# Moving a quarter of the position products into the feed-forward, and the last keys' projection between the first largest scores

## The chip, the cores and the metric

The program runs on one core of one Trainium2 chip. The metric is device time in microseconds of one execution over all eight images. TensorE multiplies matrices into PSUM (eight banks), VectorE, ScalarE and GpSimd work on tiles (GpSimd in SBUF alone here), and SyncE issues transfers. Each engine runs its own list of instructions in order, and semaphores tie the lists together.

## The reference, cut to what matters

```python
# layer 0, for each of 8 images of 32x32 tokens, C = 384, 6 heads of 64
x = x + L0_conv_ref(_gn(x), ...)      # qkv with bias; scores + rel_h + rel_w; softmax; values; projection
# inside: position terms
rel_h = einsum('bhwc,hkc->bhwk', r_q, Rh)
rel_w = einsum('bhwc,wkc->bhwk', r_q, Rw)
attn = attn + rel_h[:, :, :, :, None] + rel_w[:, :, :, None, :]
# layer 1
t = t + L1_attn_ref(_ln_t(t), Wq, Wk, Wv, Wo, bo)      # causal
t = t + L1_ffn_ref(_ln_t(t), ...)                       # kron-factored feed-forward with gelu
```

## The kernel before

Images are worked one after the other, and each has the same stages: values and position products of layer 0, attention 0, its projection and a norm, attention 1, its projection, feed-forward. The head of an image is overlapped with the feed-forward of the image ahead of it: class `Projections` computes the queries and keys of the next image in six *pairs* (two heads each; pairs 0 to 2 queries, 3 to 5 keys), 18 matmuls of 512 columns a pair. Numbers are kept as a high f16 part and a low f16 part: ScalarE writes the high part from PSUM (`pair_high`, L574), VectorE the low part (`pair_low`, L591). GpSimd writes transposed copies of the queries, high and low, for the column positions (`turn_all`, L617, into `hT` and `lT`), since GpSimd can only read what the other two have already put into SBUF.

The feed-forward is a loop of twelve steps. Step i is `ff.up` (two matmuls, L1303) into banks 0 and 1, then the gelu on ScalarE (L1315), which has to end before the next `ff.up`, since both use one bank pair. `FILL` says how many matmuls of the next image's pairs TensorE puts into each step, `HIGHS` after which gelus ScalarE evicts them. After the odd steps from 3 on comes `ff.down` (L1323), and at step 9 a first `ff.spread` (L1337).

The position products (`rel_products`, L653) come in four quarters, n = 0 to 3, of 96 small matmuls, and each fills two banks. ScalarE takes each quarter out in four pieces (`rel_high`, L670) and VectorE in four more (`rel_low`, L676). `with_v` says behind which tile of values (`v_products`, L688 and L693; ScalarE takes a tile out in L700 and L701, GpSimd makes its low part in L705) a quarter stands: 0 to 3, all behind the feed-forward. Two bank pairs alternate, so quarters 2 and 3 wait for the low parts of the quarters before.

Then come the sixteen products of the first head's *largest scores* (L825), one bank each, reduced by VectorE (L971). Their list is `attn0.prologue`, their banks are `ahead`, here four. Next, a row of maxima is turned (L830), copied by VectorE (L979), carried into `qc` by a transfer (L1063), and the first score tile (L861 to L872) and its exponential (L947) follow. The attention then runs at its own pace. Every list is written out by hand in `tensor`, `scalar`, `vector`, `gpsimd` and `sync`.

## Time and profile before

| what | us |
|---|---|
| median of 3 runs | 2881.56 |
| lowest and highest | 2880.02, 2882.01 |
| the profiled execution | 2876.72 |
| its span, first to last instruction | 2874.7 |
| TensorE busy | 2648.2 (92%) |
| ScalarE, VectorE, GpSimd busy | 2047.1, 1987.1, 1734.9 |

Times inside the trace count from the span's start. The kernel has seven boundaries between images; the sixth, around 2130 to 2215 us, is the one read closely below. A busy TensorE is not one at its peak: matmuls overlap, and a matmul's own duration holds some pipeline time.

### The profile page before, as it was taken

The page shows a single profiled execution, that of the slowest core. Times are in us where ns is not written, and L with a number is a line of the kernel's source. Part 1 is how long each engine was busy: PE and PEld are TensorE (multiplying, and loading weights), DVE is VectorE, ACT ScalarE, POOL GpSimd, SP SyncE. Part 2 cuts the span into 40 slices and gives each one's busy share as a digit, 9 for nine tenths or more (in the row PEclk, how much of TensorE's full clock was granted, in tenths as well). Part 3 has the DMA queues.
Part 4 walks back from the last instruction along what each step waited for, and adds up shares of the span by engine and source line. Part 5 has one row for each costly group of instructions (what it writes and reads, how often), then busy time and mean ns, then how long its engine had stood idle before and what let it go on. Part 6 is the DMA issues. An engine that isn't in the chain of part 4 may idle for free.

```text
span 2874.7 us, 69176 instructions
## 1 busy us (share of the span) xinstructions
PE 2648.2 (92%) x29116; PEld 1548.0 (54%) x29116; DVE 1987.1 (69%) x3631; ACT 2047.1 (71%) x2435; POOL 1734.9 (60%) x1181
## 2 busy tenths in 40 slices
PE   7899998999989998999989999899998999989995
PEld 4465644656446563565635656366553655546562
DVE  7776767666775767757677576775777758677574
ACT  6686866858668586785767867678766777668683
POOL 5474764737657376573756746566565665657473
PEclk8999999999999999999999999999999999999998
DMA  3100011000100001000010000200002000010000
GB/s 113 36 2 1 2 34 45 2 1 2 56 23 2 1 2 56 23 2 1 2 57 23 2 1 6 74 2 2 1 9 71 2 2 1 12 45 2 1 2 22
DMA packets 36115, 53.65 MB, mean 19 GB/s; under 512 B 5824, under 2 KB 32704, under 8 KB 35808
## 3 DMA queue, kind: packets, MB, share of 16 engines
q1 hardware_dynamic: 34304, 48.64, 5.5%
q8 instruction: 231, 3.78, 0.5%
q10 hardware_dynamic: 1504, 0.61, 0.1%
q14 instruction: 76, 0.62, 0.1%
HBM read 30.95 MB, written 12.58 MB: 15 GB/s over the span
## 4 chain that ended last, share of the span: by engine, by line
PE 49%; POOL 16%; ACT 13%; issue 11%; DVE 9%; DMA 1%; POOLq 0%; ACTq 0%; DVEq 0%; SPq 0%
POOL pl L1013 15%; PE ps L555 12%; PE ps L902 7%; PE ps L688 4%; PE ps L861 4%; PE ps L872 4%; ACT p L947 4%; PE ps L825 4%; PE ps L1104 4%; DVE mxp L971 3%; PE ps L863 3%; ACT ph L933 3%; ACT qa L670 2%; PE ps L1303 2%; PE ps L1323 2%
## 5 line engine op out<-in xcount | busy, mean ns | idle before, releaser
L1013 POOL TENSOR_TENSOR pl<-p,ph 128x1024 f16<-128x1024 f32 (+2 forms) x672 | 1095.9, 1644 | 384.2 <-ACT ph L933 378.3
L971 DVE TENSOR_REDUCE mxp<-ps 128x1 f32<-128x512 f32 (+2 forms) x1344 | 779.4, 627 | 267.9 <-PE ps L825 263.3
L947 ACT ACTIVATE p<-ps 128x1024 f32<-128x1024 f32 (+1 forms) x672 | 640.3, 953 | 165.8 <-PE ps L872 165.0
L933 ACT ACTIVATE ph<-p 128x1024 f16<-128x1024 f32 (+1 forms) x672 | 669.3, 996 | 21.4
L902 PEld LDWEIGHTS ps<-v,ph 128*128 128x128 f16 x9600 | 506.2, 97 | 128.2 <-issue 27.6
L902 PE MATMUL ps<-v,ph 128*128 128x65 f16 (+1 forms) x9600 | 531.0, 194 | 17.0 <-POOL pl L1013 16.0
L902 PE MATMUL ps<-v,pl 128*128 128x65 f16 x4800 | 509.1, 192 | 0.0
L902 PEld LDWEIGHTS ps<-v,pl 128*128 128x128 f16 x4800 | 446.8, 99 | 0.0
L872 PE MATMUL ps<-qc,kc 65*128 65x512 f16 (+3 forms) x1344 | 380.0, 364 | 0.1
L1013 DVE TENSOR_TENSOR pl<-p,ph 128x512 f16<-128x512 f32 (+1 forms) x336 | 244.2, 727 | 184.3 <-ACT ph L933 183.0
L705 POOL TENSOR_TENSOR v<-o,v 128x384 f16<-128x384 f32 x128 | 116.7, 918 | 411.0 <-ACT o L701 411.0
L861 PE MATMUL ps<-qa,ka 128*128 128x512 f16 x768 | 292.5, 381 | 0.0
L863 PE MATMUL ps<-qb,ka 128*128 128x512 f16 x768 | 291.7, 380 | 0.0
L825 PE MATMUL ps<-ka,qa 128*128 128x512 f16 x768 | 247.1, 383 | 43.9 <-DVE mxp L971 25.1
L700 ACT ACTIVATE v<-ps 128x384 f16<-128x384 f32 x128 | 63.6, 497 | 180.8 <-PE ps L693 107.3
L872 PEld LDWEIGHTS ps<-qc,kc 65*128 65x128 f16 (+1 forms) x1344 | 123.8, 98 | 126.4 <-issue 0.5
L825 PEld LDWEIGHTS ps<-ka,qa 128*128 128x128 f16 x768 | 73.2, 97 | 182.7 <-DVE mxp L971 70.8
L861 PE MATMUL ps<-qa,qb 128*128 128x512 f16 (+1 forms) x576 | 162.0, 344 | 2.1 <-ACT p L947 2.1
L555 PE MATMUL ps<-xin,wqkv_hi 128*128 128x512 f16 x576 | 155.9, 384 | 4.0 <-DVE xin L508 2.2
L825 PE MATMUL ps<-qb,qa 128*128 128x512 f16 (+2 forms) x576 | 154.9, 325 | 0.0
L1000 DVE TENSOR_TENSOR lT<-ps,hT 128x512 f16<-128x512 f32 x96 | 66.4, 692 | 127.5 <-ACT hT L938 127.5
L1315 ACT ACTIVATE p<-ps 128x1024 f32<-128x1024 f32 x96 | 98.0, 1021 | 60.6 <-PE ps L1303 59.5
(187 smaller groups left out, 5075.2 us busy)
## 6 DMA issues: line engine op xcount, KB each, us to landing
xin<-in_x SPq DMA_DIRECT2D x8, 1536.0 KB, 6.9
x<-in_x SPq DMA_DIRECT2D x8, 1536.0 KB, 8.1
out<-x SPq DMA_DIRECT2D x16, 768.0 KB, 4.1
qc<-qa SPq DMA_DIRECT2D x42, 128.0 KB, 2.3
p<-in_L_conv_qkv_w SPq DMA_DIRECT2D x3, 576.0 KB, 10.6
qc<-rowt SPq DMA_DIRECT2D x96, 2.0 KB
x<-in_L_attn_Wq SPq DMA_DIRECT2D x1, 576.0 KB, 7.9
x<-in_L_attn_Wk SPq DMA_DIRECT2D x1, 576.0 KB, 9.0
```

The source lines that it names most:

```text
L555: mm = nc.tensor.matmul(m.ps[:, self.bank[i] + j, :], w[:, k, self.order[i] * P:(self.order[i] + 1) * P], x(k, 4 * j, 4 * j + 4), start=(n ...
L688: mm = nc.tensor.matmul(m.ps[:, 6 + t % 2, 0:C], flat_tile(x(k, t, t + 1)), w[:, k, 2 * C:3 * C], start=(n == 0), stop=(self.layer == 1 an ...
L705: self.nc.gpsimd.tensor_tensor(self.m.v[:, t, :, HD + 1:VW], self.m.o[:, t, :].rearrange("p (h d) -> p h d", d=HD), self.m.v[:, t, :, 0:HD ...
L825: mm = nc.tensor.matmul(m.ps[:, bank, 0:w], m.qa[:, sl, qt * P:(qt + 1) * P], self.ka[:, sl, kh * BANK:kh * BANK + w], start=not diag, sto ...
L861: nc.tensor.matmul(outs[j], self.ka[:, sl, keys[j]], m.qa[:, sl, q], start=True, stop=False)
L863: nc.tensor.matmul(outs[j], self.ka[:, sl, keys[j]], m.qb[:, sl, q], start=False, stop=False)
L872: mm = nc.tensor.matmul(outs[j], m.kc[crows(h), sl, keys[j]], m.qc[crows(h), sl, q], start=False, stop=True)
L902: mm = nc.tensor.matmul(m.ps[:, 6 + half % 2, c0:c0 + w], e, v, start=(first and n == 0), stop=(g in self.last_of_half and n == len(work) ...
L933: self.nc.scalar.activation(m.ph[:, i % RING, :, 0:w], m.p32[:, i % RING, :, 0:w], ACT.Copy).then_inc(self.s["hi"], 1)
L947: nc.scalar.activation(m.p32[:, i % RING, :, 0:w], m.ps[:, 2 * (i % 2):2 * (i % 2) + 2, 0:w], ACT.Exp, scale=SCALE).then_inc(s["exp"], 1)
L971: nc.vector.reduce_max(m.mxp[:, h % 2, kh, qt:qt + 1], m.ps[:, bank, 0:w], AX.X).then_inc(s["free"], 1)
L1013: engine.tensor_tensor(m.pl[:, i % RING, part, 0:w], m.p32[:, i % RING, part, 0:w], m.ph[:, i % RING, part, 0:w], ALU.subtract).then_inc(s ...
```

## The change

For every image but the first:

- Quarter 0 of the position products goes from behind the feed-forward to step 9 of it (`REL_STEP`), ahead of `ff.down`; its four ScalarE pieces go behind gelus 9, 10, 11 and 11 (`REL_HIGHS`), its VectorE pieces between `o2_out` and `widen`.
- Pair 5, the last two heads' keys, leaves the feed-forward (`FILL` has 36 matmuls in place of 54). Its 18 matmuls stand two by two behind the first nine of the sixteen largest-score products. ScalarE writes its high parts and then the whole sums to `p32` (`last_keys_out`), GpSimd its low parts (`last_keys_low`).
- Values tile 5 stands in thirds behind the next three products, tile 6 behind all sixteen.
- The quarters use three bank pairs (`REL_BANK`), and the sixteen products two banks, 0 and 1.
- ScalarE loads the exponential's table ahead of time (`table`).
- GpSimd's first high transposes wait for the queries' high part alone.

```diff
-        self.bank = (4, 6, 2, 4, 2, 4) if layer == 0 else (0, 2, 4, 6, 0, 2)
-        self.before = (0, 0, 0, 2, 6, 8) if layer == 0 else (0, 0, 0, 0, 2, 4)
+        self.bank = (4, 6, 2, 4, 2, 2) if layer == 0 else (0, 2, 4, 6, 0, 2)
+        self.before = (0, 0, 0, 2, 6, 0) if layer == 0 else (0, 0, 0, 0, 2, 4)
...
+    def last_keys_out(self, act):
+        i = 2 * NPAIR - 1
+        f = self.order[i]
+        self.pair_high(act, i)
+        self.nc.scalar.activation(self.held_keys(), self.out2(i), ACT.Identity, bias=self.m.bqk[:, f:f + 1]).then_inc(self.late["whole"], 1)
...
+    def last_keys_low(self, pool, done):
+        m = self.m
+        pool.wait_ge(self.late["whole"], self.late.at("whole", 1))
+        pool.wait_ge(self.s["v_lo"], self.s.at("v_lo", done))
+        for h in (NH - 2, NH - 1):
+            self.nc.gpsimd.tensor_tensor(m.kc[own(h), slot(h), :], self.held_keys()[own(h), :], self.ka[own(h), slot(h), :],
+                                         ALU.subtract).then_inc(self.s["late_lo"], 1)
...
         for p in range(NPAIR):
-            pool.wait_ge(s["lo"], s.at("lo", 2 * p + 2))
-            for part in range(2):
+            for part, ready in enumerate(("hi", "lo")):
+                pool.wait_ge(s[ready], s.at(ready, 2 * p + 2))
...
+    REL_BANK = (4, 2, 0, 4)
...
-        if n >= 2:
-            pe.wait_ge(s["rel_lo"], s.at("rel_lo", 4 * (n - 1)))
+        if n == 3:
+            pe.wait_ge(s["rel_lo"], s.at("rel_lo", 4))
         if n == 0:
             pe.wait_ge(s["turned_hi"], s.at("turned_hi", NH))
             pe.wait_ge(s["turned_lo"], s.at("turned_lo", NH))
...
-        ahead = (4, 5, 0, 1, 2, 3) if self.causal else (4, 5, 2, 3)
+        ahead = (4, 5, 0, 1, 2, 3) if self.causal else (0, 1)
...
+    def table(self, act):
+        self.nc.scalar.activation(self.m.idle[:, :], self.m.bqk[:, 0:1], ACT.Exp, scale=0.0)
...
-            w.with_v = ((0,), (1,), (2,), (3,), (), (), (), ()) if b else ((), (), (0,), (1,), (2,), (3,), (), ())
+            w.with_v = ((1,), (2,), (3,), (), (), (), (), ()) if b else ((), (), (0,), (1,), (2,), (3,), (), ())
...
-        FILL = (0, 5, 5, 5, 5, 5, 5, 5, 5, 5, 5, 4)
-        HIGHS = (1, 2, 4, 5, 8, 9, 11, 11)
+        FILL = (0, 5, 5, 5, 5, 4, 4, 4, 4, 0, 0, 0)
+        HIGHS = (1, 2, 4, 5, 8, 9)
+        REL_STEP = 9
+        REL_HIGHS = (9, 10, 11, 11)
+        BESIDE_MAX = 9
...
+            pe.wait_ge(qkv0.s["rel_hi"], qkv0.s.at("rel_hi", RELS))
+            pe.wait_ge(qkv0.s["rel_lo"], qkv0.s.at("rel_lo", RELS - 4))
+            for u in attn0.prologue:
+                attn0.use(pe, u)
+                n = u[2]
+                if before and n < BESIDE_MAX:
+                    qkv0.pair_products(pe, PAIRS - 1, part=(EACH * n // BESIDE_MAX, EACH * (n + 1) // BESIDE_MAX))
+                elif before and n < BESIDE_MAX + NC_:
+                    qkv0.v_products(pe, NT - 3, [n - BESIDE_MAX])
+            qkv0.v_products(pe, NT - 2)
...
+                if i == REL_STEP and w.next:
+                    pe.wait_ge(after.s["lo"], after.s.at("lo", 2 * PAIRS - 4))
+                    after.rel_products(pe, 0)
...
             if w.next:
+                pool.wait_ge(proj1.s["rstd"], proj1.s.at("rstd", 2))
                 w.next.qkv0.turn_all(pool)
```

The order on TensorE at the end of the first feed-forward, from step 8, before: `ff.up`, five filling matmuls, step 9, `ff.down`, `ff.spread`, step 10.

```order
L1303 MATMUL ps<-ph,c 128x512 x2
L555 MATMUL ps<-xin,wqkv_lo 128x512
L555 MATMUL ps<-xin,wqkv_hi 128x512 x4
L1303 MATMUL ps<-ph,c 128x512 x2
L555 MATMUL ps<-xin,wqkv_lo 128x512 x2
L555 MATMUL ps<-xin,wqkv_hi 128x512 x3
L1323 MATMUL ps<-p,cp 32x512 x4
L1337 MATMUL ps<-spread,pl 128x32 x4
L1303 MATMUL ps<-ph,c 128x512 x2
```

The same place after the change, steps 8 and 9 to the first matmuls of quarter 0 (L678, 96 in all):

```order
L1339 MATMUL ps<-ph,c 128x512 x2
L556 MATMUL ps<-xin,wqkv_hi 128x512 x2
L556 MATMUL ps<-xin,wqkv_lo 128x512 x2
L1339 MATMUL ps<-ph,c 128x512 x2
L678 MATMUL ps<-qa,rel_hi 32x96 x2
L678 MATMUL ps<-hT,rel_hi 32x96 x2
```

And behind the last of the 96, up to the values' first matmul:

```order
L678 MATMUL ps<-hT,rel_lo 32x96 x2
L1359 MATMUL ps<-p,cp 32x512 x4
L1373 MATMUL ps<-spread,pl 128x32 x4
L1339 MATMUL ps<-ph,c 128x512 x4
L1359 MATMUL ps<-p,cp 32x512 x4
L713 MATMUL ps<-wqkv_hi,xin 128x384
```

Quarter 0, which reads GpSimd's copies `hT` and `lT`, now stands ahead of the third-last `ff.down`, and steps 10 and 11 have no filling work between them. The largest scores on TensorE, before, where a tile of values stands in one piece between six and ten of them:

```order
L825 MATMUL ps<-ka,qa 128x512 x6
L688 MATMUL ps<-wqkv_hi,xin 128x384
L688 MATMUL ps<-wqkv_lo,xin 128x384
...
L693 MATMUL ps<-bv,ones 128x384
L825 MATMUL ps<-ka,qa 128x512 x10
L830 MATMUL ps<-minus,mxp 8x128
```

After, from the eighth of them to the row's turning:

```order
L851 MATMUL ps<-ka,qa 128x512
L556 MATMUL ps<-xin,wqkv_hi 128x512 x2
L851 MATMUL ps<-ka,qa 128x512
L556 MATMUL ps<-xin,wqkv_lo 128x512 x2
L851 MATMUL ps<-ka,qa 128x512
L713 MATMUL ps<-wqkv_hi,xin 128x384
...
L718 MATMUL ps<-bv,ones 128x384
L851 MATMUL ps<-ka,qa 128x512 x4
L713 MATMUL ps<-wqkv_hi,xin 128x384
...
L856 MATMUL ps<-minus,mxp 8x128
```

The pair's matmuls and a tile of values went in between, and one whole tile of values now stands between the last of the sixteen and the row.

## Rows read from the trace of the kernel before

**Rows 1.** The page's busy times, TensorE: us, share, instructions.

```profile
PE 2648.2 (92%) x29116; PEld 1548.0 (54%) x29116; DVE 1987.1 (69%) x3631; ACT 2047.1 (71%) x2435; POOL 1734.9 (60%) x1181
```

**Rows 2.** Windows: busy us of each engine, granted clock; largest scores, then row to exponential.

```profile
core 0: us, PE busy (x) PEld busy (x) DVE busy (x) ACT busy (x) POOL busy (x), PEclk, DMA share, GB/s
...
2195.80:2206.40 10.60, 6.85 (x26) 2.27 (x26) 9.92 (x17) 2.97 (x7) 2.62 (x3) 1.00 0.01 2
2206.40:2212.30 5.90, 5.63 (x20) 2.08 (x20) 2.45 (x4) 2.22 (x4) 0.89 (x1) 0.71 0.16 30
```

**Rows 3.** Timeline of TensorE, steps 8 to 10, quarter 0: start, us, instruction, [idle before].

```profile
2166.16 1.02 PE L555 MATMUL ps<-xin,wqkv_hi 128*128 128x512 f16 x4
2167.22 0.60 PE L1303 MATMUL ps<-ph,c 96*128 96x512 f16 x2
...
2168.83 1.07 PE L1323 MATMUL ps<-p,cp 128*32 128x512 f32 x8
...
2170.74 0.60 PE L1303 MATMUL ps<-ph,c 96*128 96x512 f16 x2
...
2179.14 0.22 PE L653 MATMUL ps<-qa,rel_hi 64*32 64x96 f16 x2 [0.24 <-DVE kc L591]
```

**Rows 4.** Timelines of VectorE and GpSimd, sixth boundary: low parts, first and last of six transposes.

```profile
2148.75 7.86 DVE L591 SCALAR_TENSOR_TENSOR qb<-ps,bqk,qa 64x1024 f16<-64x1024 f32 x6
...
2151.44 3.94 POOL L617 TENSOR_SCALAR hT<-qa 64x1024 f16<-64x1024 f16 x2 [7.36 <-DVE qb L591]
...
2171.46 3.93 POOL L617 TENSOR_SCALAR lT<-qb 64x1024 f16<-64x1024 f16 x2
```

**Rows 5.** Timeline of ScalarE, sixth boundary: first and last of four quarters taken out.

```profile
2180.39 3.28 ACT L670 ACTIVATE qa<-ps 32x768 f16<-32x768 f32 x4 [1.62 <-PE ps L653]
...
2192.98 3.28 ACT L670 ACTIVATE qa<-ps 32x768 f16<-32x768 f32 x4
```

**Rows 6.** Timelines of three engines, sixth boundary: largest scores, row, scores, exponential.

```profile
2195.82 1.56 PE L825 MATMUL ps<-ka,qa 128*128 128x512 f16 x5 [0.91 <-DVE qb L676]
...
2206.49 0.38 PE L830 MATMUL ps<-minus,mxp 128*8 128x128 f32 x2 [2.29 <-DVE mxp L1006]
...
2209.95 0.61 PE L861 MATMUL ps<-qa,ka 128*128 128x512 f16 x1
...
2196.25 9.89 DVE L971 TENSOR_REDUCE mxp<-ps 128x1 f32<-128x512 f32 x16 [0.48 <-PE ps L825]
...
2207.11 1.92 DVE L676 TENSOR_TENSOR qb<-ps,qa 32x768 f16<-32x768 f32 x2
...
2210.94 1.28 ACT L947 ACT_TABLE_LOAD   x1
2212.24 1.02 ACT L947 ACTIVATE p<-ps 128x1024 f32<-128x1024 f32 x1
```

**Rows 7.** Windows in the first image: an idle stretch of TensorE, then a values tile.

```profile
61.40:64.30 2.90, 0.00 (x0) 0.00 (x0) 2.89 (x8) 2.88 (x5) 0.00 (x0) 0.87 0.00 0
64.30:67.50 3.20, 3.19 (x18) 1.36 (x22) 3.20 (x4) 0.72 (x2) 3.07 (x1) 0.58 0.03 5
```

**Rows 8.** Transfer of a row in the last image: its issue, and who waited for it.

```profile
2742.20 5.94 SPq L1063 DMA_DIRECT2D qc<-rowt  x2
...
2745.67 0.11 PEld L872 LDWEIGHTS ps<-qc,kc 65*128 65x128 f16 x2 [0.47 <-DMA qc<-rowt]
```

**Rows 9.** VectorE's copies in the first image, beside a GpSimd transpose and without one.

```profile
50.34 0.75 DVE L596 COPY qc<-qa 64x1024 f16<-64x1024 f16 x1
...
61.48 1.53 DVE L262 COPY ka<-ka 64x1024 f16<-64x1024 f16 x4
```

**Rows 10.** First boundary, three timelines: step 9, the last transpose, first largest score, first exponential.

```profile
409.02 0.60 PE L1303 MATMUL ps<-ph,c 96*128 96x512 f16 x2
...
411.84 3.92 POOL L617 TENSOR_SCALAR lT<-qb 64x1024 f16<-64x1024 f16 x2
...
437.63 1.56 PE L825 MATMUL ps<-ka,qa 128*128 128x512 f16 x5 [0.25 <-DVE qb L676]
...
454.53 1.02 ACT L947 ACTIVATE p<-ps 128x1024 f32<-128x1024 f32 x1
```

More of the change, by code:

```diff
@@ L1525, in scalar, with vector @@
                         w.next.qkv0.pair_high(act, 2 + n // 2, (n % 2,))
-        def vector(dve, w):
+                for r in range(4):
+                    if REL_HIGHS[r] == i and w.next:
+                        w.next.qkv0.rel_high(act, r)
+        def vector(dve, w, before):
             qkv0, attn0, proj0, ln, qkv1, attn1, ff = w.qkv0, w.attn0, w.proj0, w.ln, w.qkv1, w.attn1, w.ff
-            for r in REL_ORDER[:-2]:
+            for r in range(4 if before else 0, RELS - 2):
                 qkv0.rel_low(dve, r)
@@ L1612, in _ @@
                 prologue.scalar(act)
-                for w in work:
-                    scalar(act, w)
+                for b, w in enumerate(work):
+                    scalar(act, w, work[b - 1] if b else None)
             @block.vector
```

72 lines of the change are left out of this document (49 added, 23 removed).

## The prediction

> **What bounds the kernel now.** I read the page first, then the timelines of all engines around one boundary. TensorE is busy 92% of the span and every other engine 60 to 71% [rows 1], so work taken off the others pays only where TensorE waits. Two such places are in the head of an image.
>
> The first is the position quarters. Quarter 0 starts at 2179.14 [rows 3]. ScalarE takes a quarter out in 3.28 us, and the first starts at 2180.39, the fourth at 2192.98 [rows 5]. That is 12.59 / 3 = 4.20 us a quarter, the values' eviction included. VectorE follows it, and the first largest score waits for VectorE until 2195.82 [rows 6]. ScalarE is what is late there.
>
> The second is from the largest scores to the first exponential. VectorE reduces sixteen banks in 9.89 us, 0.62 each. TensorE has one matmul for each, then idles 2.29 us until the row at 2206.49 [rows 6]. The granted clock is 1.00 during the scores and 0.71 between the row and the exponential [rows 2], so part of that stretch runs at 1.2 GHz in place of 2.4. The exponential starts at 2212.24, behind a table load of 1.28 us from 2210.94 on [rows 6]. From first score to exponential: 16.42 us here, 454.53 - 437.63 = 16.90 at the first boundary [rows 10]. I take the mean, 16.66, for all seven.
>
> **The change part by part.** All times are the sixth boundary's; + is later than before.
>
> *The feed-forward up to step 9.* Steps 5 and 7 each lose one matmul of (1.02 - 0.38) / 3 = 0.21 us [rows 3]. The even steps already wait for the gelu and gain nothing, and one gelu stands behind an eviction, so of 0.43 us I keep 0.3. Step 9's `ff.up` starts at 2167.22 - 0.30 = 2166.92, and TensorE is free two matmuls, 0.43 us, later: 2167.4.
>
> *The wait for GpSimd's copies.* Quarter 0 needs all twelve transposes. They run without a break from 2151.44 to 2171.46 + 3.93 = 2175.39 [rows 4]. The change lets the first pair's two high transposes (3.94 us and 0.08 to the next) run in the 7.36 us that GpSimd idles. The low ones of that pair cannot follow earlier, since they need the first two of VectorE's six low parts, 2148.75 + 7.86 / 3 = 2151.37 [rows 4]. So the last transpose ends at 2175.39 - 4.02 = 2171.37. TensorE stands still for 2171.4 - 2167.4 = 4.0 us, where nothing was waited for before. Queued behind this wait are `ff.down`, `ff.spread` and step 10, and with them ScalarE's gelus 10 and 11.
>
> *From quarter 0 to quarter 1.* The quarter itself takes about 1.2 us of TensorE (to ScalarE's first piece it is 2180.39 - 2179.14 = 1.25 [rows 3, 5]): 2172.6. `ff.down` and `ff.spread` take 2170.74 - 2168.83 = 1.91 [rows 3]. Step 10 starts at 2174.5, +3.75. Four filling matmuls of step 11 go (-0.86, or with rounding -0.96), and the 0.24 us that quarter 0 waited for VectorE's low part of pair 5 [rows 3] goes. What then stands behind `ff.spread` is quarter 1, at +2.55. The ScalarE pieces of quarter 0 lie in time that waits for TensorE; only the second delays gelu 11, by 0.1. VectorE has as much work between `widen` and `o2_out` as before.
>
> *The clock.* After an idle stretch of 2.9 us in the first image, the 3.2 us of work behind it ran at a granted clock of 0.58 [rows 7]: it lost 3.2 x (1 - 0.58) = 1.34 us. The idle time here, 4.0 us, is longer, so I take a fall at each boundary. Part of the low stretch may pass within the wait itself, so I take 1.25; the bounds are 0 and 1.7, half of the 3.4 us of work between the end of the wait and step 10's end. The Trainium skill, "TensorE: Matmul & The Clock Gate", section "HAM oscillation — how this bites in real kernels", tells of a kernel whose every wait for a transfer sends the clock down and makes the work behind it start slow. By it each of the seven waits costs, as the term above has it, and the trace agrees [rows 7]; without it the sum would be 8.75 us lower. Nothing else here rests on it.
>
> *The quarters behind the feed-forward.* Quarter 1's eviction starts at 2180.39 + 2.55 + 1.25 = 2184.2. Three quarters remain: 2 x 4.20 + 3.28 = 11.68, to 2195.9. The products now wait for ScalarE's last piece, not for VectorE's fourteenth. First largest score at 2195.95, **+0.1**: the quarter saved on ScalarE (4.2 us) is what the wait and the clock in the feed-forward have cost.
>
> *The largest scores.* TensorE has for each of nine scores three matmuls of 0.216, 0.65 us, against VectorE's 0.62; TensorE becomes the slower by 0.03. Then three scores with a third of the values (0.7, 0.7, 0.86), and four at VectorE's pace. Two banks are enough for this: a product is ready 0.4 us after its bank is free, and VectorE has 0.62 us of work in the other. The last score is issued 9.8 us behind the first, VectorE and its combining end at 11.2, and the tile of values between last score and row (ten matmuls of 384 columns, 0.16 each) ends at 9.8 + 0.2 + 1.65 = 11.65. Row at 11.65 in place of 10.67 (2206.49 - 2195.82 [rows 6]): +1.0.
>
> *From row to exponential.* TensorE was busy all along, so I take full clock. The row's result is copied by VectorE at 12.35. Then come its two position low parts of 1.92 us [rows 6], for which the scores wait: 14.25; four score matmuls, to 15.1. The row's transfer is issued at 12.4. In one place a transfer issued at 2742.20 let its reader start at 2745.67, 3.47 us later, after 0.47 us of waiting for it [rows 8]; the other end, unseen, is that it lands before 15.1. I take 3.1 us: 15.5. Last two matmuls and their end 0.64, and the table is already loaded: exponential at **16.15**, bounds 15.75 and 16.5. Against 16.66 that is -0.5. Late keys: ScalarE's 3.3 us begin at the ninth score and end before the row; GpSimd's two subtractions end before its first low part of the attention is due. I cost both at nothing; if they were late, the fourth exponential would wait, eight us further on.
>
> *The first boundary.* Step 9 is at 409.02 and the last transpose ends at 411.84 + 3.92 = 415.76 [rows 10], so the wait there is 411.7 - 409.15 = 2.6 us, 1.4 less: -1.8 in all. The first image has no feed-forward ahead of it; its scores lose their values in between, and its table load costs nothing: 0, within 1.
>
> **Sum.** Six boundaries at +0.1 - 0.5 = -0.4 give -2.4, and the first -1.8: -4.2 us. The profiled execution took 2876.72 (span 2874.7), so 2872.5; it was 0.17% faster than the median of 2881.56, against which I forecast 2881.56 - 4.2 = **2877.4**. That is 0.15% faster, within the 0.2% (5.8 us) under which a measurement of this kernel does not tell a difference.
>
> **Rivals.** (a) *The wait costs no clock*, since the low stretch falls into the wait itself. Then -1.25 x 7: 2868.6. Against it: rows 7, where a shorter idle stretch was paid in full. For it: the low stretch there began before TensorE resumed (granted 0.87 in the idle window). If half the boundaries escape, 2873. (b) *There is hardly a wait*, because transposes and TensorE meet earlier than I read. Then the 4.0 us go too, some 5 us a boundary: 2842 to 2850. Only a GpSimd faster than its 1.96 us a transpose could do that; nothing shows it. (c) *Slower: GpSimd's early transposes slow VectorE's small operations* on the statistics, six of them, right ahead of the feed-forward, where GpSimd idled [rows 4]. A copy on VectorE took 0.75 beside a transpose and 1.53 / 4 = 0.38 without one [rows 9]. Six times up to 0.37 is 2.2 us, less 0.25 of slack before TensorE's second transposes: up to 1.95 a boundary, +13.6 - 4.2: 2891. It decides from 10.0 / 7 = 1.4 us a boundary. Against it: those operations are tiny (32 elements a partition), so 0.1 each is as likely, 2880. The Trainium skill, "GPSIMD Engine Reference", section "8. Key points", says that GpSimd shares its SBUF interfaces with VectorE and contends with some of its operations; the two copies agree. (d) *The transfer or GpSimd's late keys end last in the head*: at most 0.35 x 7 = 2.5 more for the transfer, 2880. (e) *A second low stretch* in steps 10 and 11, which have no filling left: another 1.2 in some boundaries, up to 2886.
>
> **How the numbers follow.** The forecast, with (d) and the mild form of (c), has 0.45; its own range is 2872 to 2883. (a) has 0.25, (b) 0.05, (c) in full 0.12, (e) 0.13. Range: 2865 to 2888. It leaves out (b) and the far half of (c). Faster by over 0.2% (below 2875.8): (a), (b) and the lower edge of the forecast, 0.37. Slower by over 0.2% (above 2887.3): (c) and the end of (e), 0.17. Within 0.2%: 0.46.
>
> **What the changed kernel's profile would show.** Right: TensorE idle 4 us behind step 9's `ff.up` with a GpSimd transpose as releaser, 2.6 us at the first boundary; a low granted clock right behind it; three quarters of 3.28 us on ScalarE; some 16.1 us from first largest score to exponential, no table load ahead of it, and a clock of 1.00 there. Wrong: a wait of under 3 us (the transposes' term), quarter 1 at full clock (a), a feed-forward that begins later behind its statistics (c), or a first score that is more than 1 us off the old place relative to the feed-forward's first gelu. If the first exponential waits for GpSimd or for the row's transfer beyond 16.5, the last term is wrong.

## The result, and the profile after

The changed kernel takes 2903.43 us (median of 4 runs, 2901.4 to 2909.97) beside 2881.78 us of the kernel before on the same chip: ratio 1.0079, 95% interval 1.0062 to 1.0097. It is 0.8% slower, and lies above the range. A second set of runs on another chip gave 2903.03 us and 1.0071 (1.0044 to 1.0098). The profiled execution took 2901.4 us (span 2899.7), 24.7 more than that of before.

The page's busy times of the changed kernel, as in [rows 1]: GpSimd has 29 us more, which are its fourteen subtractions for the late keys (L627, 2.12 us each), TensorE 16, and ScalarE and VectorE 9 each.

```profile
PE 2664.2 (92%) x29116; PEld 1557.2 (54%) x29116; DVE 1996.1 (69%) x3617; ACT 2056.3 (71%) x2450; POOL 1764.3 (61%) x1195
```

The gelu's table load is a mark that stands at the same place in both kernels. From the table's own small activation I measure the first gelu and the first exponential of the next image, at every boundary. These are the marks at the sixth boundary of the changed kernel (start us, us, instruction, [idle before]): table, first gelu and first exponential from ScalarE's timeline, then the first largest score and the row from TensorE's.

```profile
2144.80 0.20 ACT L1345 ACTIVATE idle<-f2sum 128x1 f32<-128x1 f32 x1
...
2167.94 1.02 ACT L1351 ACTIVATE p<-ps 128x1024 f32<-128x1024 f32 x1 [2.60 <-PE ps L1339]
...
2230.80 1.02 ACT L983 ACTIVATE p<-ps 128x1024 f32<-128x1024 f32 x1 [0.98 <-PE ps L902]
```

```profile
2214.56 0.39 PE L851 MATMUL ps<-ka,qa 128*128 128x512 f16 x1 [1.41 <-ACT qa L695]
...
2226.69 0.39 PE L856 MATMUL ps<-minus,mxp 128*8 128x128 f32 x2
```

| behind the table, us | before, seven boundaries | changed, seven boundaries |
|---|---|---|
| first gelu | 19.65 in all | 23.14 in all |
| last transpose ends | 45.5 to 45.6 | 43.2 |
| first exponential | 82.1 to 84.3, mean 83.17 | 86.0 to 86.1, mean 86.01 |
| first exponential to the next table | mean 267.0 | mean 267.5 |

Up to the last table 23.3 us are lost: 7 x 2.84 = 19.9 in the heads and 3.8 in the middles of the images, less 0.4 in the first. The last image's feed-forward has a longer stretch at low clock and adds 1.7 (24.6 us from first to last gelu in place of 22.9). That is 25.0, the difference of the spans.

The gelus begin 3.5 us late. In the changed kernel's VectorE and GpSimd timelines the operations on the statistics (L1285, then four of L1289) stand beside the first two transposes:

```profile
2159.12 0.16 DVE L1184 SCALAR_TENSOR_TENSOR ln<-mv,ln 128x4 f32<-128x4 f32 x1 [0.21 <-POOL ln L1179]
2159.32 1.79 DVE L1285 TENSOR_SCALAR ln<-ln,f2sum 128x4 f32<-128x4 f32 x1
2161.22 2.50 DVE L1289 TENSOR_SCALAR ph<-ph,ln 128x32 f32<-128x32 f32 x4
```

```profile
2159.18 3.89 POOL L640 TENSOR_SCALAR hT<-qa 64x1024 f16<-64x1024 f16 x2
```

The same two lines of the kernel before, at its sixth boundary, where GpSimd idled:

```profile
2144.31 0.23 DVE L1249 TENSOR_SCALAR ln<-ln,f2sum 128x4 f32<-128x4 f32 x1
2144.65 0.92 DVE L1253 TENSOR_SCALAR ph<-ph,ln 128x32 f32<-128x32 f32 x4
```

An operation on four elements a partition took 1.79 us in place of 0.23. It ends at 2161.11, where the first transpose ends (2159.18 + 3.89 / 2 = 2161.1). The group of four took 2.50 in place of 0.92, all of it in the first. That is no slower pace: each lasts until the GpSimd instruction beside it is over. I call this the *hold*; it shows as the operation's own duration, not as a wait.

The kernel before had the same hold at the same boundary, a few operations earlier. L1138, another operation on four elements a partition, took 0.98 us beside a GpSimd instruction of 1.00, in each of the eight images, and 0.17 without one:

```profile
2134.91 0.98 DVE L1138 TENSOR_SCALAR ln<-mv 128x4 f32<-128x4 f32 x1
...
2142.82 0.17 DVE L1138 TENSOR_SCALAR ln<-mv 128x4 f32<-128x4 f32 x1
```

```profile
2134.87 1.00 POOL L1236 TENSOR_TENSOR o<-x,cf 128x384 f32<-128x384 f32 x1 [0.51 <-DVE x L1125]
```

In the changed kernel TensorE stands still for 2.14 us behind the held L1289, and again for 2.23 us at step 9:

```profile
2163.16 0.90 PE L1314 MATMUL ps<-ident,ph 128*32 128x128 f32 x4 [2.14 <-DVE ph L1289]
...
2185.33 0.60 PE L1339 MATMUL ps<-ph,c 96*128 96x512 f16 x2 [0.25 <-ACT p L1351]
...
2188.16 0.26 PE L678 MATMUL ps<-qa,rel_hi 64*32 64x96 f16 x2 [2.23 <-POOL lT L640]
```

Windows of the same boundary (busy us of each engine, granted clock in the column PEclk): the two idle stretches, the work behind each, a third low stretch, and the largest scores up to the exponential.

```profile
core 0: us, PE busy (x) PEld busy (x) DVE busy (x) ACT busy (x) POOL busy (x), PEclk, DMA share, GB/s
2161.30:2163.10 1.80, 0.00 (x0) 0.00 (x0) 1.80 (x2) 1.11 (x1) 1.76 (x1) 1.00 0.00 0
2164.35:2167.65 3.30, 3.30 (x9) 1.06 (x7) 2.95 (x4) 0.96 (x2) 0.00 (x0) 0.50 0.14 29
2185.90:2188.10 2.20, 0.03 (x1) 0.00 (x0) 1.28 (x1) 2.17 (x3) 2.04 (x2) 1.00 0.00 0
2188.20:2191.50 3.30, 3.30 (x104) 2.06 (x104) 0.00 (x0) 1.05 (x2) 0.00 (x0) 0.50 0.02 5
2195.05:2198.35 3.30, 3.30 (x14) 0.88 (x14) 2.87 (x3) 2.70 (x4) 2.62 (x2) 0.50 0.02 5
2214.60:2230.80 16.20, 15.04 (x73) 6.73 (x74) 12.65 (x20) 8.89 (x15) 7.43 (x6) 1.00 0.23 73
```

Each idle stretch had a clock of 1.00, and the work behind it 0.50, 1.2 GHz. There are three such stretches in each of the seven feed-forwards that a next image follows, the third behind only 1.12 us of idleness; in the kernel before, the first boundary's had one and the other six none. The last window answers [rows 2]: from first score to exponential the clock is 1.00 now, as meant.

So there are two suspects: the hold, at the place of rival (c), and the wait at step 9 with the clock behind it. Which of them costs the time is not in this trace, since both stand in every boundary. Executions that ran several per cent longer than the others of their kernel are left out of all numbers below: two of four in e8_delay, two of ten in e2, one of ten in e10 and one of five in e12.

### The profile page after: what moved, and what is told of

Read it like the earlier page. It is cut to its first block, busy times and chain, and to the rows that moved or that the text cites. A ratio compares the mean times of both kernels' runs of the same rounds, so it can differ in the third digit from the quotient of the medians.

```text
span 2899.7 us, 69244 instructions
## 1 busy us (share of the span) xinstructions
PE 2664.2 (92%) x29116; PEld 1557.2 (54%) x29116; DVE 1996.1 (69%) x3617; ACT 2056.3 (71%) x2450; POOL 1764.3 (61%) x1195
## 4 chain that ended last, share of the span: by engine, by line
PE 45%; POOL 18%; ACT 15%; issue 11%; DVE 10%; DMA 0%; POOLq 0%; ACTq 0%; DVEq 0%; SPq 0%
POOL pl L1049 15%; PE ps L556 10%; PE ps L932 7%; PE ps L851 4%; PE ps L713 4%; PE ps L889 4%; PE ps L902 4%; ACT p L983 4%; PE ps L891 3%; ACT ph L963 3%; ACT qa L695 2%; DVE stats L1165 2%; DVE x L1161 2%; ACT p L1351 2%; PE ps L1140 2%
## 5 line engine op out<-in xcount | busy, mean ns | idle before, releaser
L851 PE MATMUL ps<-ka,qa 128*128 128x512 f16 x768 | 255.7, 386 | 44.8 <-DVE mxp L1007 22.2
```

The costliest lines, as they stand in the source:

```text
L851: mm = nc.tensor.matmul(m.ps[:, bank, 0:w], m.qa[:, sl, qt * P:(qt + 1) * P], self.ka[:, sl, kh * BANK:kh * BANK + w], start=not diag, sto ...
```

## The experiments

All kernels but e2 are edits of the changed kernel. Ratios are to the kernel before on the same chip, with 95% intervals. "Idle" is TensorE's idle time right ahead of quarter 0, "first exponential" the mean over seven boundaries of the time behind the gelu's table, both in the profiled execution. The experiments ran in batches on several chips, so kernels of different batches are compared by their ratios.

| kernel | median us | ratio | idle | first exponential |
|---|---|---|---|---|
| before | 2881.78 | 1 | 0.24 | 83.2 |
| changed | 2903.43 | 1.0079 (1.0062 to 1.0097) | 2.2 | 86.0 |
| e1_gate | 2904.32 | 1.0069 (1.0050 to 1.0088) | 2.7, six times 4.0 | 84.2 |
| e2_early_alone | 2894.9 | 1.0044 (1.0026 to 1.0062) | | 85.5 |
| e3_split | 2904.03 | 1.0072 (1.0050 to 1.0095) | 2.7, six times 4.0 | 85.8 |
| e4_form | 2905.59 | 1.0078 (1.0054 to 1.0102) | | 85.7 |
| e5_warm | 2878.66 | 0.9996 (0.9987 to 1.0005) | 0.1 | 82.5 |
| e6_step10 | 2850.89 | 0.9896 (0.9881 to 0.9910) | 0 to 1.65 | 77.8 |
| e6_step11 | 2845.98 | 0.9882 (0.9868 to 0.9897) | 0 | 77.8 |
| e7_step11_open | 2868.89 | 0.9948 (0.9930 to 0.9967) | 0 | 80.5 |
| e8_delay | 2904.3 and 2905.4 | | | 86.0 |
| e9_delay2 | 2911.3 | 1.0092 (1.0068 to 1.0115) | | 87.9 |
| e10_late_turns | 2885.7 | 0.9997 (0.9982 to 1.0012) | 2.3 to 3.9 | 82.8 |
| e11_warm9 | 2883.14 | 1.0003 (0.9989 to 1.0018) | 0.1 to 0.4 | 83.1 |
| e12_warm_x2 | 2901.7 | 1.0069 (1.0042 to 1.0096) | 3.9 | 86.0 |
| e13_warm_both | 2882.62 | 0.9999 (0.9984 to 1.0013) | 1.8 | 83.6 |
| after_again | 2903.03 | 1.0071 (1.0044 to 1.0098) | | 86.2 |

### What the hold is

**e1_gate.** The first transposes only behind the last x2:

```diff
                 pool.wait_ge(proj1.s["rstd"], proj1.s.at("rstd", 2))
+                pool.wait_ge(ff.s["x2"], ff.s.at("x2", 8))
```

> The changed kernel with one wait more: GpSimd starts the transposes of the next image's queries only when VectorE has written the last of the eight x2 (L1289). Theory 1 (VectorE's statistics operations are held while a GpSimd transpose runs, and that holds the feed-forward): L1285 and the first L1289 take 0.23 and 0.30 us again instead of 1.79 and 1.88, the gelu table stands 19.6 to 19.7 us ahead of the first gelu instead of 23.1, seven boundaries give 7 x 3.4 = 24 us back, and the time is 2878 to 2882. Theory 2 (the loss is made at step 9, by the wait for the transposes and the clock that falls after it, and the late start of the feed-forward only hides a part of it): the feed-forward starts 3.4 us earlier but waits 5.7 us at step 9 instead of 2.25, since the last transpose ends where it did; the time stays at 2898 to 2904. What decides between them is whether the last transpose ends earlier too: the first theory says yes, since its GpSimd work waits for VectorE's lower parts, which follow the start of the feed-forward.

The hold went, the first gelu stood at 19.65 again, and the time did not move. The last transpose ends at 41.6 in place of 43.2, only 1.6 earlier, and TensorE waits 4.05 us instead of 2.23. The first exponential of the third boundary is at 86.1, as in the changed kernel. TensorE at that boundary, and windows of the wait and of the work behind it:

```profile
1118.73 0.60 PE L1339 MATMUL ps<-ph,c 96*128 96x512 f16 x2 [0.25 <-ACT p L1351]
1123.39 0.26 PE L678 MATMUL ps<-qa,rel_hi 64*32 64x96 f16 x2 [4.05 <-POOL lT L640]
```

```profile
1119.40:1123.30 3.90, 0.00 (x0) 0.00 (x0) 1.27 (x1) 2.42 (x3) 3.76 (x2) 0.76 0.00 0
1123.40:1129.90 6.50, 6.50 (x114) 3.94 (x114) 0.66 (x1) 0.80 (x1) 0.00 (x0) 0.50 0.01 3
1129.90:1134.90 5.00, 3.88 (x14) 0.77 (x14) 4.28 (x5) 4.33 (x5) 3.58 (x2) 0.50 0.00 0
```

Here the clock is at its lower level for over 11 us of work, where the changed kernel had 6.8. What the hold gave back, the clock took. Theory 2 had the time (2904.32 against 2904 at most); theory 1 was right that the last transpose ends earlier. The last four boundaries of the same execution had a low stretch of 6.8 us and their exponentials at 83.4; that execution took 2889.74 us, all the others 2900.6 to 2906.5, so the table's mean of 84.2 stands for the fastest one only.

**e2_early_alone.** The kernel before with the early high transposes and nothing else:

```diff
-            pool.wait_ge(s["lo"], s.at("lo", 2 * p + 2))
-            for part in range(2):
+            for part, ready in enumerate(("hi", "lo")):
+                pool.wait_ge(s[ready], s.at(ready, 2 * p + 2))
...
             if w.next:
+                pool.wait_ge(proj1.s["rstd"], proj1.s.at("rstd", 2))
                 w.next.qkv0.turn_all(pool)
```

> The kernel before with one part of the change alone: GpSimd may turn the upper parts of a pair of queries as soon as they stand, without waiting for the lower parts, from when the second half's root is written. Theory 1 (held statistics operations): the feed-forward of seven boundaries starts 3.4 us later, and the time rises by about 24 us, to 2902 to 2908; nothing in this kernel reads the turned queries early, so nothing is gained. Theory 2 (the loss comes from the quarter at step 9): the time is that of the kernel before, 2880 to 2884.

It loses 0.44%, about 13 us, with nothing else of the change present, and half of what theory 1 asked. L1249 took 1.79 us again. The first gelu came 1.8 us late at two boundaries and 3.4 at five. In the five the granted clock fell behind TensorE's 2.13 us of idleness, in the two it did not: so at the first gelu the hold is worth 1.8 us, and the clock behind it another 1.6. A part is taken up later, since the first exponential is 2.3 us late on average.

**e3_split.** The first two transposes in eight pieces each:

```diff
         dst, src = self.turned(part, p, parity)
+        if part == 0 and p == 0 and self.late:
+            for n in range(7):
+                self.nc.gpsimd.tensor_scalar(dst[:, 4 * n:4 * n + 4, :], src[:, 4 * n:4 * n + 4, :], 1.0, 0.0, ALU.mult, ALU.add)
+            dst, src = dst[:, 28:32, :], src[:, 28:32, :]
```

> The changed kernel with each of the first two transposes of a boundary, 1.9 us long, cut into eight instructions of an eighth of the rows each. Theory 1a (a VectorE operation is held until the GpSimd instruction in flight has ended): L1285 and the first L1289 are held for no more than one piece each, some 0.3 to 0.5 us in place of 1.79 and 1.88, the feed-forward starts 2.5 to 3 us earlier than in the changed kernel, and the time is 2880 to 2886. Theory 1b (the two engines share a port and slow each other as long as both have work): cutting changes nothing, L1285 and L1289 end when the last piece does, and the time stays within 5 us of 2903.

VectorE and GpSimd at its seventh boundary (the lines are four further down):

```profile
2515.26 0.28 DVE L1289 TENSOR_SCALAR ln<-ln,f2sum 128x4 f32<-128x4 f32 x1
2515.65 1.36 DVE L1293 TENSOR_SCALAR ph<-ph,ln 128x32 f32<-128x32 f32 x4
```

```profile
2515.12 2.58 POOL L642 TENSOR_SCALAR hT<-qa 64x128 f16<-64x128 f16 x7
```

0.28 in place of 1.79 beside pieces of 0.39 us, and 1.36 for the four in place of 2.50. Each operation ends within 0.07 us of a piece's end, and the first gelu is at 19.65. That settles the hold: it lasts to the end of one GpSimd instruction (1a), and is no shared bandwidth (1b). It has a price on the other side: the two transposes last from 2515.12 to 2521.75, 6.6 us in place of 3.9, which delays nothing here. The time did not move here either, with 4.0 us of waiting at six boundaries and 13.7 us of low clock at each of them.

**e4_form.** The two operations with two inputs in SBUF, same arithmetic:

```diff
-        nc.vector.tensor_scalar(m.ln[:, 2, half], m.ln[:, 2, half], m.f2sum[:, 0:1], None, ALU.mult).then_inc(s["offset"], 1)
+        nc.vector.tensor_tensor(m.ln[:, 2, half], m.ln[:, 2, half], m.f2sum[:, 0:1].broadcast_to([P, 4]), ALU.mult).then_inc(s["offset"], 1)
...
-            nc.vector.tensor_scalar(self.x2[:, t, :], self.x2[:, t, :], m.ln[:, 1, t:t + 1], m.ln[:, 2, t:t + 1], ALU.mult, ALU.add).then_inc(s["x2"], 1)
+            nc.vector.scalar_tensor_tensor(self.x2[:, t, :], self.x2[:, t, :], m.ln[:, 1, t:t + 1], m.ln[:, 2, t:t + 1].broadcast_to([P, FA]), ALU.mult, ALU.add).then_inc(s["x2"], 1)
```

> The changed kernel with another form of the two statistics operations on VectorE: L1285 and L1289 read their second operand as a tensor (a column broadcast) instead of as a scalar, so that they have two inputs, as L1184 and L1327 have; the arithmetic is the same. GpSimd still turns the first queries at once. Theory 1c (only forms with one input in SBUF are held by a running GpSimd instruction): L1285 and L1289 take 0.2 to 0.4 us each while the transposes run, the feed-forward starts 19.7 to 20 us behind the gelu table, and the time is 2875 to 2884. Theory 1d (any VectorE operation on SBUF is held, and the forms that were seen running free had their source in PSUM or met no transpose): both still last to the end of a transpose, and the time stays at 2900 to 2906.

```profile
739.90 1.78 DVE L1285 TENSOR_TENSOR ln<-ln,f2sum 128x4 f32<-128x4 f32 x1
741.79 2.38 DVE L1289 SCALAR_TENSOR_TENSOR ph<-ph,ln 128x32 f32<-128x32 f32 x4
```

Held all the same, so 1c falls. Theory 1d is right for these forms, but not for *any* operation on SBUF: VectorE's sum L1277 (TENSOR_REDUCE `ph<-o`, SBUF to SBUF) takes 0.54 us in the changed kernel whether it starts within a GpSimd instruction of 1.00 us (L1272, 40 times) or beside none. An operation that starts just before the transpose (L1184, 0.16) is not held. Operations with a source in PSUM are not either: VectorE's low parts (L592) take 1.29 us beside transposes and 1.28 without.

### What the wait costs

**e5_warm.** e1 with 18 products of 128x512 into the wait. Nobody reads them, and they write to a bank that the quarter overwrites:

```diff
+                    after.idle_products(pe, 18)
                     after.rel_products(pe, 0)
```

> e1_gate with the wait at step 9 filled: 18 products of 128x512 into the banks that the quarter overwrites afterwards stand ahead of the quarter, 18 x 0.21 = 3.7 us of TensorE work that nothing reads, where TensorE idled 4.06 us. No wait goes and none is added, so what changes is the granted clock alone. Theory A (the loss of the changed kernel without the hold is the low clock that follows the wait): the quarter takes 1.20 us instead of 2.10 and the down products 1.07 instead of 1.93, the first gelu stands 61 to 62 us ahead of the first exponential instead of 63.7 to 66.4, and the time is 2860 to 2870. Theory B (the chain over GpSimd's transposes and ScalarE sets the time, and TensorE's clock in this stretch lies beside it): the time stays with e1_gate, 2898 to 2905.

No wait was removed, and the ratio fell from 1.0069 to 0.9996: 0.73%, 21 us, 3.0 a boundary, which only the granted clock can have given. Windows of the filled wait and of the work behind it, at the third boundary:

```profile
1111.50:1115.50 4.00, 3.91 (x19) 1.55 (x16) 1.27 (x1) 2.50 (x3) 3.84 (x2) 1.00 0.00 0
1115.50:1119.50 4.00, 3.64 (x114) 2.26 (x114) 0.69 (x1) 1.06 (x2) 0.00 (x0) 1.00 0.01 4
```

Theory B falls. Theory A had the mechanism and promised at least 9 us too much: at five of seven boundaries a low stretch of 3.4 us came later, 46.7 to 48.3 behind the table. At the two without one the first exponential is at 81.2.

**e6_step10, e6_step11.** e1 with the quarter one or two steps later; the second is:

```diff
-        REL_STEP = 9
-        REL_HIGHS = (9, 10, 11, 11)
+        REL_STEP = 11
+        REL_HIGHS = (11, 11, 11, 11)
```

> e1_gate with the quarter one step of the feed-forward later (behind the up products of step 10 instead of step 9; ScalarE's copies of it behind the gelus of steps 10 and 11). The transposes end 41.65 us behind the gelu table in e1_gate and step 10 is reached at about 39.9, so that 1.5 to 2 us of the wait of 4.06 stay. Theory A (idle TensorE and the low clock behind it): less idle time and a shorter low stretch, 2862 to 2880. Theory B (GpSimd's chain and ScalarE's copies set the time): the copies come later, and the time is that of e1_gate or up to 2 us a boundary above, 2900 to 2915.

> e1_gate with the quarter two steps later, behind the up products of step 11, and all four ScalarE copies behind the last gelu. The last transpose (41.65 us behind the table) should stand before TensorE comes to the quarter at about 41.5 to 43, so that no wait is left. Theory A: no idle time over 0.5 us ahead of the quarter, no low clock in the last steps of the feed-forward, 2855 to 2872. Theory B: all four copies (0.80 us each) now stand behind the last gelu, and the time is at or above that of e1_gate, 2898 to 2915.

Both beat the kernel before, by 1.0 and 1.2%, and both come out below the range that theory A gave. With step 11, TensorE at the third boundary goes from the step's `ff.up` into the quarter without a stop:

```profile
1104.91 0.60 PE L1339 MATMUL ps<-ph,c 96*128 96x512 f16 x2 [1.18 <-ACT p L1351]
1105.44 0.22 PE L678 MATMUL ps<-qa,rel_hi 64*32 64x96 f16 x2
```

```profile
1100.50:1105.50 5.00, 3.64 (x28) 1.46 (x31) 3.41 (x4) 4.27 (x5) 4.70 (x4) 1.00 0.00 0
1105.50:1112.50 7.00, 7.00 (x223) 4.05 (x226) 5.52 (x7) 5.10 (x7) 3.44 (x2) 1.00 0.32 115
```

The quarter starts at 41.9 here and at three more boundaries, hardly later than in e1 (41.8), and at 43.3 at the other three, where a low stretch came at 22. But `ff.down`, `ff.spread` and steps 10 and 11, which were queued behind the wait, are done by then. That is what the later place buys: the wait of 4 us is filled with work that has to be done. At those four boundaries the first exponential is at 77.2, against the 81.2 of e5: 4.0 us. All four ScalarE pieces stand behind the last gelu, and ScalarE still waits 0.64 us for TensorE behind them, so they are not what is late.

**e7_step11_open.** e6_step11 without its gate, the hold alone.

> e6_step11 without its gate: GpSimd turns the first upper parts at once, so that VectorE's L1285 and the first L1289 are held again (1.79 and 1.88 us), and the quarter stands behind step 11, where the last transpose (43.0 us behind the table in the changed kernel) is there before TensorE comes (about 45.4). The hold by itself, with no wait at step 9 that could take it up. Theory E (the hold has its full price once nothing behind it waits for GpSimd): seven times 1.8 us where the granted clock does not fall in TensorE's 2.1 us of idleness, 3.4 us where it does, so 12 to 24 us above the 2846 of e6_step11: 2858 to 2870. Theory F (the hold is hidden behind ScalarE and VectorE later in the feed-forward, and in the changed kernel it was the wait alone that cost): 2844 to 2850.

Ratio 0.9948 against 0.9882 of e6_step11: 0.66%, 19 us, and the first exponential 80.5 in place of 77.8, 2.7 a boundary, part of it clock that falls behind the hold. Theory E. So the same hold costs 19 us where nothing behind it waits for GpSimd, while taking it away brings nothing (e1) where the wait at step 9 follows. Its last transpose is at 43.3, like the changed kernel's.

**e10_late_turns.** Step 11, and both parts of a pair turned behind its low parts, as before the change.

> e6_step11 with the transposes as they were before the change: GpSimd turns both parts of a pair only when its lower parts stand, with no gate. It starts at 21.6 instead of 15.9 us behind the table, so that twelve transposes of 2.0 us end at 45.5 us instead of 41.6. If the early start of the first two is what lets the quarter in (theory G), the quarter begins 3.6 us later than in e6_step11 and the clock falls behind the wait: 7 x 3.6 to 5.5 us, 2871 to 2885. If the rest of the head takes the wait up (theory H: the copies of ScalarE and VectorE are what sets the first largest score), the time is 2845 to 2855.

Ratio 0.9997 against 0.9882: 33 us, 4.7 a boundary, theory G. The last transpose is at 45.6, TensorE waits for it again and the clock falls behind it. Without the early start of the two transposes the quarter's place in the feed-forward gains nothing over the kernel before.

**e11_warm9, e12_warm_x2, e13_warm_both.** The changed kernel, with 10 products in the idle stretch at step 9, ahead of the second half of x2's transposes, or in both.

```diff
             ff.x2_transposes(pe, 0)
             if w.next:
                 after.pair_products(pe, 2, part=(0, SECOND))
+            if w.next:
+                after.idle_products(pe, 1, 10)
             ff.x2_transposes(pe, 1)
...
+                    after.idle_products(pe, 4, 10)
                     after.rel_products(pe, 0)
```

> The changed kernel, hold and all, with 10 products of 128x512 that nothing reads in the 2.25 us in which TensorE waits at step 9. Only the granted clock can change. Theory A (the low clock behind the wait is on the path): quarter 2.10 to 1.20 us, down products 1.70 to 1.07, and the second low stretch (down 1.93, V products 1.87) goes too, 3 us a boundary, 2880 to 2888. Theory B (ScalarE's and VectorE's copies are the path there): 2900 to 2905.

> The changed kernel with 10 such products in the 2.13 us in which TensorE waits for the held L1289, ahead of the second half of x2's transposes. The hold stays; the low stretch behind it should go, so that the first gelu stands 21.5 us behind the table instead of 23.1. Theory I (the wait for GpSimd at step 9 takes it up, since the last transpose does not come earlier by more than 0.3 us): 2899 to 2905. Theory J (each low stretch costs what its own products show): 1.65 us a boundary, 2890 to 2894.

> The changed kernel with both fills, 10 products each: the hold and the wait at step 9 as they are, and no low clock behind either. Theory I: the time of e11_warm9 less at most 2 us, 2878 to 2886. Theory J: 1.65 us a boundary below e11_warm9, 2868 to 2876.

e11 takes 20 us away, with nothing changed but work that nobody reads: as much as the change had lost. In the third boundary's windows the clock is 1.00 throughout:

```profile
1119.50:1125.50 6.00, 4.81 (x121) 2.53 (x124) 2.44 (x3) 3.35 (x5) 1.48 (x2) 1.00 0.01 3
1125.50:1132.50 7.00, 7.00 (x139) 3.79 (x131) 6.62 (x8) 4.40 (x7) 2.69 (x3) 1.00 0.33 116
```

The same `ff.down` products in the changed kernel at half clock, and in e11:

```profile
2190.20 1.71 PE L1359 MATMUL ps<-p,cp 128*32 128x512 f32 x8
...
2195.00 1.93 PE L1359 MATMUL ps<-p,cp 128*32 128x512 f32 x8
```

```profile
1120.92 1.07 PE L1363 MATMUL ps<-p,cp 128*32 128x512 f32 x8
...
1125.08 1.07 PE L1363 MATMUL ps<-p,cp 128*32 128x512 f32 x8
```

e12 brings the first gelu from 23.1 to 21.5 and gains nothing: TensorE waits for GpSimd longer by the same amount, and the first exponential stays at 86.0 (theory I).

```profile
1123.11 0.26 PE L682 MATMUL ps<-qa,rel_hi 64*32 64x96 f16 x2 [3.93 <-POOL lT L644]
```

e13 is e11 within the interval (theory I again). It still idles 1.8 us at step 9 behind its ten products, and at all seven boundaries keeps its clock there; at three a low stretch comes later, at 48.4 to 49.2.

### Is the period a sum?

From table to table the changed kernel takes 355.0 us six times within 0.1 (the last time 344.9). In e3 five periods are 354.97 to 355.00, although the hold is gone. I suspected that the low stretches hold the period at fixed lengths, so that a delay would be free.

**e8_delay.** The first exponential of each later image twice.

> The changed kernel with a known delay on the path of each boundary: the first exponential of the first attention is done twice, 1.0 to 1.2 us more, right behind the row on which everything waits; the result is the same. Theory C (the periods are held at 355.0 us from boundary to boundary by where the low-clock stretches fall, which is why seven of seven periods agree within 0.1 us and why taking the hold away gave nothing): the delay is taken up elsewhere in the period, and the time stays within 3 us of 2903. Theory D (the period is the sum of its parts): seven times 1.0 to 1.2 us, 2910 to 2913.

2905.4 and 2904.3 us, but it does not decide. In its timeline the second exponential starts 3.29 us behind the first, as in the changed kernel, so the extra one lay in a gap:

```profile
1169.84 1.02 ACT L984 ACTIVATE p<-ps 128x1024 f32<-128x1024 f32 x1 [0.98 <-PE ps L902]
1170.89 1.02 ACT L986 ACTIVATE p<-ps 128x1024 f32<-128x1024 f32 x1
...
1173.13 1.02 ACT L986 ACTIVATE p<-ps 128x1024 f32<-128x1024 f32 x1
```

**e9_delay2.** Five idle products ahead of the largest scores of each later image.

> The changed kernel with 5 products of 128x512 that nothing reads ahead of the first largest score of each later image, 1.07 us on a path on which nothing waits for GpSimd (the extra exponential of e8_delay was not on the path: the second one started at its old time). Theory C (the period is held at 355.0 us by where the low-clock stretches fall): the periods stay at 355.0, and the time within 3 us of 2903. Theory D (the period is the sum of its parts): each period is 1.07 us longer, and the time 2908 to 2914.

2911.3 lies in the range of D, but the ratio is only 0.13 to 0.21% above the changed kernel's, 4 to 6 us of the 7.5 that were put in, and its interval holds both: in the total it leans to the sum and does not decide. Boundary by boundary it is no sum: four periods are 355.1 to 355.4, as if the delay were free, and the next two 358.5. At the latter the low stretch behind step 9's wait lasts 13.7 us, at the former 3.4 and 3.4. At the former the delay is not free in the head, where the first exponential is 0.8 to 1.1 us late, but most of it comes back in the middle of the image: from first exponential to next table 268.3 us in place of the changed kernel's 269.0, because a low stretch 148 us behind the first exponential is absent. Windows there, behind the third boundary of the changed kernel and of e9:

```profile
1313.85:1318.85 5.00, 4.84 (x20) 2.67 (x21) 2.02 (x4) 4.13 (x7) 1.14 (x2) 0.66 0.01 3
```

```profile
1315.23:1320.23 5.00, 4.28 (x27) 2.76 (x28) 1.96 (x4) 4.22 (x8) 1.56 (x2) 1.00 0.01 3
```

So a delay shifts which low stretches come: over a whole period it was worth 0.1 to 0.4 us or 3.5.

**after_again** is the changed kernel beside e11 to e13.

> The changed kernel itself, unchanged, beside the three others on the same chip: 2901 to 2906, seven periods of 355.0 us.

2903.03, and periods of 355.0 but for the first two (356.6 and 354.8). At its first boundary TensorE idled the same 2.13 us behind the hold, and the clock stayed at 1.00 behind it; the first gelu came at 21.45, and the low stretch at step 9 was one of 13.7 us.

## Why the prediction was wrong

Two terms failed, and the rest of the sum came out. Against the prediction's own steps, in the order of its text:

- *The feed-forward up to step 9*: its length was right. TensorE is free at step 9 17.99 us behind the first gelu (2185.33 + 0.60 - 2167.94); the sum had 2167.4 - 2149.4 = 18.0 behind that of before, 19.65 behind its table. Its start was wrong. The sum took the place of the first gelu as given and put GpSimd's early transposes at nothing. **This is the first step that failed**: the gelus begin 3.5 us later.
- *The wait for GpSimd's copies*: 4.0 us was forecast, and e1 and e3 measured 4.05 and 3.97 once the hold was gone. In the changed kernel 2.23 are left, since the late feed-forward took up the rest; 1.6 us of the hold come back as a later last transpose (43.2, against the 41.6 that the sum implies).
- *The clock*: right in kind, **and the second step that failed, since its term was mis-sized**. The sum had 1.25 us a boundary from one low stretch. With the idle stretch filled, e11 gets back 86.0 - 82.8 = 3.2 at six of seven boundaries: 0.9 of it on the quarter itself, and the rest on products behind it, in the stretch directly behind the wait and in another at 50.2 (rival (e), a second low stretch, which came at all seven boundaries). Without the hold it is 3.0 (e1 and e5). Of the low clock behind a wait I had priced only the work up to step 10.
- *The quarters, scores and row*: three quarters on ScalarE, a full clock and no table load ahead of the exponential. First score to row took 12.13 us (11.65 forecast), row to exponential 4.11 (4.5), together **16.24 against 16.15**. The total is right within 0.1 partly by luck: the row came 0.5 us late (the last score product started 10.08 us behind the first in place of 9.8, and the row 2.05 us behind that in place of 1.85), and the way from row to exponential was 0.4 shorter. The transfer, which had set it in the sum, was waited for by nobody: the last two products started 2.75 us after its issue, right behind the four score products, which had waited for VectorE's low part.
- *Rival (c)* named the place and the engines of the loss. Its price, up to 0.37 for each of six operations, came from the copy of 0.75 us in [rows 9], read as a copy slowed to half its pace. It was not: GpSimd's transpose beside it, the first of these two, began at 48.89 and ended at 50.81,

```profile
48.89 3.99 POOL L617 TENSOR_SCALAR lT<-qb 64x1024 f16<-64x1024 f16 x2 [0.36 <-DVE qc L596]
```

  0.47 us into the copy, and the copy ended 0.28 later. The row showed a hold cut short because the copy came late, not the size of the effect. The four copies of that group all end 0.28 us behind a transpose; one row alone could not tell it, but L1138 above, 0.98 us in place of 0.17, could have. "Those operations are tiny" was the wrong reason for a small price: what counts is how much is left of the GpSimd instruction beside, here 1.9 us.
- *The other rivals*: (a), no clock cost, and (b) did not come; (d) had no part. Of the prediction's own signs of being wrong, two came: a wait of under 3 us, and a feed-forward that begins later behind its statistics.

The ledger for one boundary, from table to first exponential: before 83.17, forecast 82.6. Without hold and without clock loss 81.2 is measured (two boundaries of e5), and the sum less its clock term gives 82.6 - 1.25 = 81.3. So the other terms held in their total. The hold adds 1.6 (e11, 82.8), the clock 3.2, and that is 86.0. The miss by these two terms is about 1.6 + (3.2 - 1.25) = 3.55 a boundary, 25 us. The heads missed by 19.9 + 4.2 = 24.1 (the first boundary, forecast at -1.8, came at 86.1 against 84.3, +1.8), of 29.2 in the spans. The rest is 3.8 us in the middles of the images and 1.7 in the last feed-forward, of which the sum had nothing, less 0.4 in the first image.

The Trainium skill, "TensorE: Matmul & The Clock Gate", section "HAM oscillation — how this bites in real kernels", tells of a kernel in which each wait sends the clock down. The changed kernel's profile agrees at all seven waits of 2.2 us at step 9, and e11 shows their price; e13's idle stretches of 1.8 us there did not send it down. On the hold, the Trainium skill's "GPSIMD Engine Reference", section "8. Key points", cited with rival (c), tells of contention alone. The page that says how long it lasts is the Trainium skill's "SBUF — State Buffer", section "SBUF: two separate sides": the port pair that VectorE and GpSimd share is a lock, and of a GpSimd operation and a VectorE operation that needs the pair (one in a 2-port perf mode or with two SBUF inputs), whichever starts first has it for the whole instruction. The trace agrees, with 1.79 and 1.88 us for operations of 0.23 and 0.30, and e3 with 0.28. By it, rival (c) would have had 1.56 + 1.58 = 3.1 us of hold less the slack; how much of that the wait at step 9 gives back would still have had to be worked out.

**What stays open.** The half microsecond that each image's middle takes longer (268.99 against 268.1 to 268.7) may lie in the place of its low stretch, 148.5 us behind the first exponential against 147.5 to 148.5; it was not tested. The length of the idle stretch alone does not say whether the clock falls: 2.13 us behind the hold kept it at two of seven boundaries of e2, three of e7 and one of after_again, and at step 9 up to 1.65 (e6_step10) and 1.8 (e13) kept it, while 1.5 at two boundaries of e4 did not. Nor does it say for how long: behind 3.9 to 4.05 us the low clock lasted 13.7 us (six boundaries of e3, two of e1), 6.8 (four of e1) or 3.4 and 3.4 (all seven of e12). Why was not found.

## What to carry to other kernels

Before GpSimd work is moved beside short VectorE operations on which others wait, read whether those work in SBUF, and look for one of the same form beside GpSimd work in the trace at hand: each can be held for as long as the GpSimd instruction beside it lasts. Cutting that into pieces or gating it took the hold away, though neither saved time as long as the wait at step 9 stood behind it. Price a wait of TensorE with the work behind it at half clock, not only with its own length; if a step needs a late input, put it behind the work that its queue would otherwise hold up (here two steps later, which with the gate turned 0.8% slower into 1.2% faster, and without it into 0.5% faster). And a cause that is real and removed may give nothing, as long as a second one right behind it takes up the slack: only the four combinations (e1, e7, e6_step11 and the changed kernel) showed what each was worth.

## What the runs showed of the hardware

- A VectorE operation of 0.23 us, on four elements a partition, took 1.79 us beside a GpSimd transpose of 1.9 us, in forms with one and with two inputs in SBUF (1.79 and 1.78). Beside GpSimd pieces of 0.39 us it took 0.28, and in the kernel before one of 0.17 took 0.98 beside a GpSimd instruction of 1.00. VectorE's low parts, with a PSUM source, were not held (1.29 beside, 1.28 without), and neither was a TENSOR_REDUCE from SBUF to SBUF (0.54 beside and without).
- TensorE's clock fell to its lower level behind idle stretches of 2.1 to 2.3 us at all boundaries of the changed kernel's profiled execution, though not behind every such stretch elsewhere (2.13 us kept it at two of seven boundaries of e2). Work that nobody reads, put into one of the two stretches, was worth 20 us.
- Around and behind a wait of 4.0 us the clock was low for 13.7 us at six of seven boundaries of e3, behind one of 2.2 us for 3.4 and 3.4, and behind one of 3.9 us (e12) for 3.4 and 3.4 too. The wait of 4.0 us filled and without low clock had the first exponential at 81.2 (e5), idle and with 13.7 us of low clock at 86.1 (e1, e3): 4.9 us, more than the wait itself.
